# Convolutions in pairs of quads, with indices and first nodes kept on the chip

## The reference

```
def mesh_conv(x, src, dst, ea, w1, b1, g, bt, w2, b2):
    m = jnp.concatenate([x[dst], x[src], ea], axis=-1) @ w1 + b1
    m = jax.nn.silu(group_norm(m, g, bt))
    m = m @ w2 + b2
    out = jax.ops.segment_sum(m, dst, num_segments=n)
    cnt = jax.ops.segment_sum(jnp.ones((dst.shape[0],), m.dtype), dst, num_segments=n)
    return out / jnp.clip(cnt, 1.0)[:, None]
```

## Time and profile before

| | |
|---|---|
| median of 3 runs | 9721.02 us |
| span of the profiled execution | 12891.0 us |
| what lies around the span | not shown by the profile |
| POOL busy | 6660.9 us, 52% |
| PE busy | 8215.0 us, 64% |
| DVE busy | 6623.8 us, 51% |
| ACT busy | 4214.8 us, 33% |
| mean busy share of the DMA engines | 3 to 4 tenths, 103 GB/s |
| mean granted clock of TensorE | 0.762 of full |

### The profile page before, as it was taken

How to read it: one execution, slowest core, us unless ns; L and a number is a source line. 1 busy time by engine, 2 the same in 40 slices (tenths; PEclk the granted TensorE clock), 3 DMA queues, 4 the chain that set the end, 5 groups by cost and what they waited for, 6 DMA issues and landing times. The chain is left out here.

```text
span 12891.0 us, 178199 instructions
## 1 busy us (share of the span) xinstructions
PE 8215.0 (64%) x44314; PEld 6512.4 (51%) x44314; DVE 6623.8 (51%) x13722; ACT 4214.8 (33%) x19386; POOL 6660.9 (52%) x6618
## 2 busy tenths in 40 slices
PE   2656656665556666666466666566547778887775
PEld 1434434444344444444355555455437777777774
DVE  4656656666556666665644444444553333333335
ACT  0333333333233333333122222222213333333332
POOL 4555555563456655655155555555315555555551
PEclk7777777777777777777677777777757777787886
DMA  3333333332333333333344444444334444444443
GB/s 104 97 88 96 96 94 93 98 99 67 92 91 99 97 96 96 100 95 93 93 137 137 136 136 137 134 139 137 105 80 95 93 96 94 95 96 95 96 98 90
DMA packets 1712639, 1324.75 MB, mean 103 GB/s; under 512 B 623557, under 2 KB 1489166, under 8 KB 1711480
## 3 DMA queue, kind: packets, MB, share of 16 engines
q1 hardware_dynamic: 1471910, 772.17, 22.1%
q0 software_dynamic: 237088, 539.87, 16.3%
q10 hardware_dynamic: 2610, 1.32, 0.1%
HBM read 1252.35 MB, written 60.09 MB: 102 GB/s over the span
## 5 line engine op out<-in xcount | busy, mean ns | idle before, releaser
L544 POOL DMA_INDIRECT conv_gath<-b,idx x3232 | 3346.9, 1036 | 2600.7 <-DMA conv_n<-in_n_b 1440.5
L896 POOL DMA_INDIRECT gat_gath<-g,idx x1616 | 1604.6, 993 | 1745.6 <-DVE gat_val L1138 1056.1
L896 POOL DMA_INDIRECT attn_gath<-kv,idx x1616 | 1584.8, 981 | 1478.9 <-DVE attn_val L1138 816.5
L578 PE MATMUL conv_sums<-conv_hot,conv_m 128*128 128x128 f32 x6464 | 1173.9, 336 | 1777.1 <-ACT conv_m L628 1075.1
L578 PEld LDWEIGHTS conv_sums<-conv_hot,conv_m 128*128 128x128 f32 x6464 | 1059.3, 241 | 2083.5 <-ACT conv_m L628 1144.7
L616 ACT ACTIVATE acc<-conv_sums,acc 128x1 f32 x3232 | 849.0, 263 | 2442.6 <-remote 1744.4
L664 DVE TENSOR_REDUCE conv_var<-conv_sq 128x32 f32<-128x512 f32 x808 | 550.6, 681 | 1509.3 <-ACT conv_sq L608 1099.9
L566 PEld LDWEIGHTS conv_z<-conv_win,conv_hotT 128*128 128x128 f32 x6464 | 984.9, 216 | 641.5 <-issue 641.2
L562 PE MATMUL conv_z<-conv_wblock,conv_ea 128*128 128x512 f32 x1616 | 1014.8, 715 | 220.6 <-issue 107.7
L1014 ACT COPY small<-attn_smalls 40x127 f32 x1616 | 420.0, 260 | 2123.2 <-remote 1207.6
L566 PE MATMUL conv_z<-conv_win,conv_hotT 128*128 128x128 f32 x6464 | 984.2, 298 | 156.3 <-issue 155.6
(11 more groups left out here) (356 smaller groups left out, 16190.9 us busy)
## 6 DMA issues: line engine op xcount, KB each, us to landing
conv_win<-a SPq DMA_DIRECT2D x3232, 64.0 KB
conv_places<-places SPq DMA_DIRECT2D x202, 512.0 KB
attn_win<-q SPq DMA_DIRECT2D x1616, 64.0 KB
gat_xeT<-in_xeT SPq DMA_DIRECT2D x404, 256.0 KB
conv_gath<-b,idx POOLq DMA_INDIRECT x3232
attn_places<-places SPq DMA_DIRECT2D x101, 512.0 KB
gat_places<-places SPq DMA_DIRECT2D x404, 128.0 KB
attn_gath<-kv,idx POOLq DMA_INDIRECT x1616
```

What stands on the lines that cost most here:

```text
L544: pool.indirect_dma_start(gath[:, b.c * BQ + k, t, :], None, b_table, bass.IndirectOffsetOnAxis(ap=idx[:, b.c, k * QT + t:k * QT + t + 1], ...
L578: mm = nc.tensor.matmul(sums[so][:, t * P:(t + 1) * P], m[:, k, t * P:(t + 1) * P], hot[:, k, t, :], start=True, stop=True)
L896: pool.indirect_dma_start(gath[:, b.c * BQ + k, t, :], None, table, bass.IndirectOffsetOnAxis(ap=idx[:, b.c, k * QT + t:k * QT + t + 1], a ...
```

## The change

All source indices and all first nodes are loaded once, in the first node stage, into a tensor `plan` of 128 x 3232 int32:

```
+            if kind == "first":
+                sp.dma_start(C["src"], w["src_b"][0, :, :]).then_inc(plan_landed, 16)
+                sp.dma_start(C["n0"], w["n0_b"]).then_inc(plan_landed, 16)
...
+def starts_of(nc, C, engine, b):
+    _, starts = nc.values_load_multi_w_load_instructions(
+        C["n0"][:, b.i * TB:(b.i + 1) * TB], engines=(engine,), min_val=0, max_val=N,
+        skip_runtime_bounds_check_because="destinations are node numbers")
+    return starts
```

With that the transfers of indices and first nodes in the convolution and attention edge stages go, and so do POOL's wait for them and SP's wait for `placed`:

```
             def gather(b, *_):
-                if b.q:
-                    pool.wait_ge(meta_landed[b.c], FIRST + b.q * META)
                 for k in range(BQ):
...
-            def fetch(b, nxt, _):
-                if nxt:
-                    fetch_starts(nxt)
+            def fetch(b, *_):
                 done(sp, z_ready, (b.i - RB + 1) * BQ)
-                done(sp, hot_ready, (b.i - RB + 1) * BQ)
-                done(sp, placed, 2 * ((b.i - RB) * TB + 1))
-                if b.q:
-                    sp.dma_start(idx[:, b.c, :], w["src_b"][0, :, bass.ds(b.i * TB, TB)]).then_inc(meta_landed[b.c], 16)
+                done(sp, hot_ready, (b.i - RC + 1) * BQ)
```

More of the change, by code:

```diff
@@ L491, in conv_edges @@
         win_landed = [st.sem(f"win_landed{n}") for n in range(WQ)]
-        starts_landed = [st.sem(f"starts_landed{c}") for c in range(RB)]
         hotT_ready, hot_ready, var_ready, normed, u_ready = (
@@ L571, in pre_activation, with sum_up @@
                 mm.then_inc(z_ready, 1)
-            def sum_up(b, k):
-                so, g = k % SQ, b.quad(k)
+            def sum_up(g):
+                if not 0 <= g < NQ:
+                    return
                 done(pe, m_ready, g + 1)
@@ L778, in attention_edges @@
         idx = C["idx"]
-        starts_in = st.sb("starts_in", [1, RB, TB], I32)
-        n0 = st.sb("n0", [1, RB, TB], I32)
+        if gat:
+            left = C["plan"][0:1, (WQ + LQ // 2) * QE:(WQ + LQ // 2) * QE + 2 * RB * TB]
+            starts_in, n0 = (left[:, n * RB * TB:(n + 1) * RB * TB].rearrange("p (c t) -> p c t", t=TB) for n in range(2))
         cols = st.sb("cols", [P, RB, 2 * TB])
@@ L890, in gather @@
             def gather(b, *_):
-                if b.q:
+                if gat and b.q:
                     pool.wait_ge(early_landed[b.c], FIRST + b.q * EARLY)
@@ L1402, in _ @@
             sp.wait_ge(stored[1], NGRP // 2 * STORES)
-            if kind != "gat":
+            if kind == "first":
+                sp.wait_ge(plan_landed, 2 * 16)
+            if kind == "attn":
                 sp.wait_ge(first_idx, RB * 16)
```

290 lines of the change are left out of this document (125 added, 165 removed).

## The result

The changed kernel takes 9804.20 us in the median of 4 runs (9795.53 to 9807.09). Beside it the kernel before took 9720.88, a ratio of 1.0085 with an interval of 1.0073 to 1.0097: slower by 0.85%, some 83 us. The forecast was 9645 us.

A forecast was written before the change was run, and what follows sets the result against it. The prediction took POOL's list of gathers to bound the timed kernel (9732 us against 9721). Its terms gave 9721 - 70 - 20 + 15 = 9646, say 9645 us, in a range of 9310 to 9776 us.

The forecast's parts named there:

- The sum of POOL's list: Whole kernel: POOL's gathers one after the other plus the node stages give 9732 us, against a median of 9721.
- the 3170 us between the two times: Whole kernel: profiled execution 12891 us against median 9721; nearly all the trace's waits were said to belong to the profiled execution.
- POOL's wait, −70: Convolutions: POOL's wait for indices goes; 70 us gained, with a lower end of 0.
- the 541 us: Edge stages: upper end of POOL's waits if all gathers took 0.94 us, which makes the floor 9180 us.
- The second rival: Convolutions: much faster, their loop holds them back when timed too and the change frees them; 9310 us, chance 0.14.
- The ends of the stages, −20: Convolution ends: less work after POOL's last gather, some 24 us in place of 45 and 42; 20 us gained.
- DVE's list, hidden: Convolutions: DVE's list grows from 17.4 to 19.0 us a batch, hidden under POOL's 21.6 us.
- POOL beside DVE, +15: Convolutions: more chain links run beside the gathers and may lengthen them; 15 us lost.
- The third rival: Convolutions: slower, DVE's two-input links beside the gathers lengthen them; 9776 to 9920 us, chance 0.14.
- threshold of 0.45 us a batch: Convolutions: POOL held up by more than this (90/202) decides against the change.
- the mark for rival 3: Profile of the changed kernel: gathers past 1100 ns would show the slower case, chance 0.14.
- The 11,500 to 12,200 us for a profiled execution: Whole changed kernel when profiled: expected span, against 12891 us before, since POOL's waits are in it.

The follow-up runs named there:

- e1: The kernel before, unaltered, profiled once more on another chip: 9700.58 us.
- e13: Changed kernel with gamma and beta read from PSUM, five z buffers, ramp in SBUF, on a slow chip: 11,940.83 us, ratio 0.9343.
- e2: Kernel before, old order by batches, with only the change's resident indices, first nodes and six cols buffers: 9697.39 us, ratio 0.9993.
- e16: The changed kernel, unaltered, measured again on another chip: 9769.41 us, ratio 1.0068.
- e4: e2 with every link of the chain done as two instructions on 64 columns, 24 links a batch: 9681.36 us, ratio 0.9955.
- e11: Changed kernel with a quad's DVE operations one behind the other and the same instructions: 9719.57 us, ratio 1.0022.
- e10: Changed kernel with five z buffers in place of six and nothing moved to PSUM: 9755.61 us, ratio 1.0059.
- e5: Changed kernel with 4 links a pair in place of 12, leaving out nearly all Newton steps: 9696.84 us, ratio 0.9977.
- e8: Changed kernel with gamma, beta and the one-hot's ramp read from PSUM in the convolutions, five z banks in place of six: 9450.37 us, ratio 0.9742.
- e12: e8 with the attention stage's ramp and softmax weights in PSUM too, for one of two smalls banks: 9358.27 us, ratio 0.9648.
- e18: e8 with DVE's list in the order of e11: 9418.77 us, ratio 0.9703.

## Why the prediction was wrong

**What bounds the kernel: right, with some luck.** The sum of POOL's list, 9732 us against 9721, named the bound, and e1 and the profile after confirm it. That it met the median to 0.1% was chance: in e1 the parts around the edge stages take 1076 us and not 1165, the gathers of attention and gat 1013 and 1039 ns and not 981 and 993, and these errors nearly cancel. And the prediction laid the 3170 us between the two times on the profiling. What was met later speaks for the chip: on that of e13 the kernel before takes 12,773 us without a profile too.

**POOL's wait, −70: wrong.** The lower end, zero, was the truth (e2: 0.9993). The prediction had said that the sum leaves none, and took 70 all the same, because some gathers take 0.94 us. Those that take longer do so in the fast trace as well: 1036 ns in the slow profile, 1031 in e1 in the convolutions, and even more in the other two stages. The mean was a property of the kernel, and the 541 us under it were no waits. The second rival stood on the same 541 us, and its sum is off besides: it says half of them and takes 0.75, where half gives 9445 us and not 9310.

**The ends of the stages, −20: right in kind, two thirds of the size.** From POOL's last gather to ACT's last accumulation e1 has 32 us and the changed kernel 26; the two parts behind lost 13 us.

**DVE's list, hidden: right in size.** A link takes 224 to 226 ns (said: 0.22), the links of a convolution add up to 194 us more and DVE's busy time, in which records overlap, grew by 139 us where 200 were expected. DVE stayed hidden: inside the convolutions POOL waits for none of it.

**POOL beside DVE, +15: the step that failed, and the one that turned the sign.** Measured are +97 us (1061 against 1031 ns), and +74 between e16 and e1. It was worked out as DVE's longer list (19.0 / 17.4) times the 55 ns between the gathers of convolutions and attention, and neither number counts. The 55 ns are 18 in e1 (1031 against 1013). Twice the links in the old order made gathers no longer (e4), and the same operations in another order took back 15 ns on one chip (e11 against e10). The cost lies in how one list of operations falls on the other: above all in gathers that meet a large operation and a link, 661 in place of 337.

The third rival, with a chance of 0.14, had the kind of mechanism. Its threshold of 0.45 us a batch was passed by the first measurement (97 / 202 = 0.48) and not by the second (74 / 202 = 0.37); the kernel is slower in both because the gains to be outweighed were 13 us and not 90. Its reason, more two-tensor links, was only half of it: in pairs taking eight links away gives the loss back (e5), in batches adding twelve doesn't cause it (e4). What it took from the rows for itself, that the longest gathers are where DVE is busiest, leaves out the gat stage: there DVE is busy for 1121 us and the attention has 1353, but its gathers are the longer ones already in the earlier trace rows (993 against 981 ns), and in e1 they are the longest of all (1039).

"Gathers keep 1000 to 1060 ns" was just missed at 1061, and the mark for rival 3, over 1100 ns, was set far too high: 30 ns in 3232 gathers with nothing to hide them decide the sign.

The Trainium skill ("SBUF — State Buffer", section "Who interferes with whom") says that a DVE instruction with at most one input in SBUF and outside the two-port modes doesn't contend with GpSimd, and that one with two inputs there does with GpSimd's reads; e8 and e12 agree, 1053 to 957 ns and 1016 to 955 ns. The same section infers that a `tensor_tensor`, though it has two such inputs, doesn't hold up the making of descriptors. These gathers are held up by it, and the measurement decides; whether by the descriptors or by the reading of the indices, no run here shows.

**The time.** 9804 lay above the range, whose upper end was the third rival with half its price and all of the gains of 90 us; the gains were some 13. Of the 159 us between forecast and measurement 70 are the wait that wasn't there, 7 the ends of the stages, and some 80 the longer gathers. The 11,500 to 12,200 us for a profiled execution weren't tested: the changed kernel was profiled only on chips of 9700 us (9803 and 9760 us).

## What to carry to other kernels

When gathers on POOL bound a kernel, look at the waits of POOL and at the mean length of its gathers: a change that touches neither its work nor its waits can still make them 2 to 3% longer in the mean. Before an order is blamed or praised, see where operands lie; one operand of DVE's large operations in PSUM gave more here (2.6% and another 1%) than the order of the list (0.4% to 0.5%), and the order in pairs was needed to afford the bank. And when the profiled execution takes a third longer than the timed ones, profile again before anything is worked out from its waits.

## What was not expected of the hardware

- The same kernel takes 9700 us on several chips and 12,773 on another, at a mean granted clock of 0.803 (e13) against 0.90 for kernels in pairs elsewhere. POOL's waits for `attn_val` and `gat_val` are 798 and 1053 us there, where elsewhere they are 11 us at most or none. In the first profile ACT started 8.3 us after PE's recorded end; that PE's results are late on such a chip is likely, and what would make them late isn't known.
- A gather of 128 rows takes 0.94 us alone, with 0.30 us ahead of it, in the convolutions as in the attention stage, whose rows are twice as long, and 1.25 us in the row above when two large operations on SBUF operands meet it. A few take far longer; the longest of e1, 5.67 us, lies at the start of the second convolution, and why isn't known.
- The order of two lists against each other, with nothing waiting, is worth 0.4% to 0.5% of this kernel (e11 against e16, e18 against e8).
